# Time-warping distances with token tiles as the array's weights, and twenty identity matmuls as TensorE's first work

## The chip, the core and the metric

The kernel runs on one core of a Trainium2 chip. The core has TensorE (matmuls and transposes into PSUM), VectorE, ScalarE, GpSimd and SyncE, which only issues transfers, and they run beside each other and meet at semaphores. The metric is the device time of the whole program in microseconds; lower is better.

## The reference, cut to what matters

A block of two parts on tokens x (2 x 2048 x 512). The first aligns 154 context rows of each batch with the 2048 layer-normed tokens by dynamic time warping and adds every context row to the tokens that the path pairs it with. The second is a mixture of 8 linear experts with the top 2 of each token.

```python
D = sqrt(maximum(aa + bb - 2.0 * a @ b.T, 0.0))       # a: 154 context rows, b: 2048 normed tokens
R[i, j] = D[i, j] + min(R[i-1, j], R[i, j-1], R[i-1, j-1])
# backtrack R from its last corner; expanded[j] += a[i] for each cell (i, j) of the path
x = x + tanh(g_xattn) * expanded
w, sel = top_k(layernorm(x) @ gate_w.T, 2)
x = x + tanh(g_ffn) * sum over sel of softmax(w) * (layernorm(x) @ expert_w[sel].T)
```

## The kernel before

Tokens lie as 32 tiles of 128, in NG = 8 groups of GT = 4 tiles (512 tokens); the width of 512 is CH = 4 pieces of 128. The groups are worked in the order `ORDER`, from both ends of each sequence inwards, since the recurrence runs from both ends at once: the 154 context rows are two halves of H = 77, the second reversed. A **unit** of distances is one half of the context (h) of one batch (b) against one group of tokens (g); `UNITS` lists all NU = 16 in the order in which they are made.

**VectorE**, for each group: four statistics (`stats`, L715 and L719), a reciprocal (L725), four normalisations of a token tile into `stage` (`norm`, L731); after each second group the squared norms of the normed tokens in three bf16 pieces (`squared_norms`, L742 to L748). Then the values of the lanes (L757 to L779, with small borders), then the recurrence.

**TensorE** turns the context (L1415) and each group of `stage` (`transposes`, L1439: 16 fp32 transposes, one a weight load and a matmul against the identity). A unit (`products`, L1463) has the context as the weights, 80 or 104 columns of them, and 512 tokens as the moving side, summed over four pieces, two instructions a product. 104 columns are the second half of the context and, from column 96, eight rows of the centred gate, so that a unit with h = 1 gives the gate's logits too. Four small bf16 matmuls (L1473) add the squared token norms to each unit, after a turn of them (`bb_turn`, L1447). In the loop TensorE has transposes of group i, then unit i - 1; after the loop the other eight units follow on each other.

**ScalarE** copies the turned tokens to `big` (L1196), takes roots of the variances (`roots`, L1150), and for each unit does a relu with the context's squared norms as bias (`distances`, L1209) and a square root (L1215), for h = 1 a copy of the gate rows too (L1218). Between the last units it lays the codes of the traceback (`codes_laid`, L1250), then the table of tanh. **SyncE** loads the tokens, writes each unit's distances to memory (`distances_out`, L438) and reads them back skewed, in chunks of CS = 8 steps (`chunk`, L450, four transfers): chunk 0 asks for 4 units written, chunk 1 for 8, chunk 2 for 12, all later ones for 16. **GpSimd** sets constants, then waits until the groups are turned and splits the context into three bf16 pieces (L568 to L579, operations of 1 to 2 us), for the alignment at the end.

**The recurrence** has NS = 108 steps of five operations on VectorE (L793 to L806; L803 is the scan that reads the distances), beside which ScalarE and TensorE make the table of moves and turn the experts' weights (1 MB each, `stage` is their buffer). Behind it come the traceback (L818 to L883), the alignment, the gate and 78 tiles of experts (L1675, L1690), to the end.

## Time and profile before

| | |
|---|---|
| median of 3 runs | 637.68 us (637.3 to 638.35) |
| profiled execution | 639.95 us, span 638.2 us |
| busy PE / DVE / ACT / POOL | 490.0 / 298.9 / 250.3 / 237.6 us |
| chain that ended last, by engine | PE 60%, DVE 28%, DMA 4%, issue 3%, ACT 2% |

PE is TensorE's matmuls and PEld its weight loads, which overlap them; DVE is VectorE, ACT ScalarE, POOL GpSimd, SPq SyncE's queue. The page's chain follows the last instruction back to what released each step. L1690 (expert matmuls) is 40% of it, the products of the distances, L1463, 8%, the recurrence and the traceback most of VectorE's share. Busy shares are averages over stages that have different limits: the chain says which engine to read in which stage.

### The profile page before, as it was taken

What the parts mean: (1) busy time and instruction counts of PE and PEld (TensorE: products, weight loads), DVE (VectorE), ACT (ScalarE), POOL (GpSimd) and SP (SyncE); (2) the same over time, 40 slices, a digit from 0 to 9 for tenths busy, and PEclk for the clock granted to TensorE, in tenths of its full rate; (3) what the DMA queues carried; (4) which work ended last, traced back from release to release, by engine and by line L of the source; (5) the groups of instructions that cost most, each with busy time, mean ns of one, the idle gap of its engine ahead of it and who ended that gap; (6) DMA issues with size and microseconds to landing.
All of it is one profiled execution on the core that took longest, in us unless ns stands there. A gap on an engine that the chain in (4) does not pass through costs nothing.

```text
span 638.2 us, 7598 instructions
## 1 busy us (share of the span) xinstructions
PE 490.0 (77%) x1994; PEld 256.9 (40%) x2006; DVE 298.9 (47%) x1522; ACT 250.3 (39%) x460; POOL 237.6 (37%) x229
## 2 busy tenths in 40 slices
PE   3899997667700000474999899999999999999994
PEld 3554334445400000233545454444445444444441
DVE  7788974999998887799982400000000000000000
ACT  3665477464420000087578523222223332222221
POOL 4002903000000000012343356686677666766742
PEclk9899999896655555585999999999999999999998
DMA  9912524970007000375977966787787778777864
GB/s 297 372 33 69 163 59 125 261 187 20 2 0 263 1 1 5 133 275 173 311 217 185 356 129 109 136 164 137 134 159 138 137 135 158 122 137 136 153 101 61
DMA packets 56107, 91.76 MB, mean 144 GB/s; under 512 B 19263, under 2 KB 19263, under 8 KB 55907
## 3 DMA queue, kind: packets, MB, share of 16 engines
q0 software_dynamic: 18016, 43.00, 36.0%
q1 hardware_dynamic: 33056, 39.03, 18.9%
q10 hardware_dynamic: 4995, 9.25, 4.7%
q8 instruction: 18, 0.29, 0.2%
q14 instruction: 22, 0.18, 0.1%
HBM read 50.05 MB, written 41.21 MB: 143 GB/s over the span
## 4 chain that ended last, share of the span: by engine, by line
PE 60%; DVE 28%; DMA 4%; issue 3%; ACT 2%; SPq 1%; POOL 0%; ACTq 0%; POOLq 0%; DVEq 0%
PE psum L1690 40%; PE psum L1463 8%; DVE met L880 5%; PE psum L1675 5%; DVE waves L803 4%; DVE tokens L883 3%; DVE tokens L818 3%; PE psum L1439 2%; DVE tokens L946 2%; DVE shf L794 2%; PE psum L1617 2%; DVE tokens L806 1%; DMA am<-in_ctx_dram 1%; DMA tokens<-x_rows,gather_ids 1%; DVE tokens L797 1%
## 5 line engine op out<-in xcount | busy, mean ns | idle before, releaser
L1690 PE MATMUL psum<-big,tokens 128*128 x624 | 282.3, 596 | 0.2 <-ACT tokens L1371 0.2
L1690 PEld LDWEIGHTS psum<-big,tokens 128*128 128x128 f32 x624 | 113.1, 191 | 114.0 <-issue 114.0
L640 POOL DMA_INDIRECT tokens<-x_rows,gather_ids x78 | 77.8, 998 | 44.8 <-issue 23.0
L653 POOL DMA_INDIRECT out_dram<-work,add_ids x40 | 65.0, 1626 | 55.8 <-DMA out_dram<-work,add_ids 19.8
L653 POOL DMA_INDIRECT out_dram<-prow,add_ids x38 | 59.9, 1576 | 46.2 <-DMA out_dram<-work,add_ids 13.4
L1381 ACT ACTIVATE work<-psum,tile_shares 128x512 f32<-128x512 f32 x40 | 27.4, 686 | 101.2 <-PE psum L1690 95.2
L660 POOL DMA_DIRECT2D out_dram<-tokens x2 | 1.8, 910 | 168.7 <-DVE tokens L946 168.7
L1381 ACT ACTIVATE prow<-psum,tile_shares 128x512 f32<-128x512 f32 x38 | 26.0, 686 | 92.1 <-PE psum L1690 92.1
L1463 PE MATMUL psum<-big,aT 128*80 128x512 f32 (+1 forms) x128 | 60.3, 602 | 0.0
L1342 ACT ACTIVATE stage<-tokens,nm 128x512 f32<-128x512 f32 x32 | 21.6, 711 | 96.6 <-DVE tokens L946 96.6
L1585 PE MATMUL psum<-side,work 128*128 128x2 f32 x8 | 1.9, 356 | 70.6 <-DVE work L905 70.6
L1675 PEld LDWEIGHTS psum<-ident,tokens 128*128 128x128 f32 x312 | 38.6, 141 | 39.8 <-issue 35.9
L1371 ACT COPY tokens<-psum 128x512 f32<-128x512 f32 x78 | 45.1, 579 | 12.5 <-PE psum L1675 12.5
L1675 PE MATMUL psum<-ident,tokens 128*128 128x128 f32 x312 | 46.9, 273 | 2.0 <-DMA tokens<-x_rows,gather_ids 1.9
L803 DVE TENSOR_TENSOR_SCAN waves<-waves,shf,tokens 128x65 f32<-128x65 f32 x108 | 38.5, 357 | 12.7 <-DMA tokens<-dist_rows 12.7
L880 DVE SCALAR_TENSOR_TENSOR met<-tokens 128x70 bf16<-128x70 bf16 x108 | 31.5, 292 | 3.8
L1504 PE MATMUL psum<-ident,stage 128*128 128x128 f32 x128 | 20.0, 308 | 13.8 <-DMA stage<-in_L_ffn_expert_w_dram 11.0
L1585 PEld LDWEIGHTS psum<-side,work 128*128 128x128 f32 x8 | 1.8, 327 | 70.7 <-DVE work L905 70.7
L1617 PE MATMUL psum<-sm,prow 128*128 128x512 bf16 x90 | 28.5, 424 | 2.3 <-DVE tokens L946 1.6
L1463 PEld LDWEIGHTS psum<-big,aT 128*80 128x80 f32 (+1 forms) x128 | 18.7, 160 | 22.6 <-issue 21.2
L793 DVE TENSOR_TENSOR waves<-waves 128x64 f32<-128x64 f32 x108 | 27.2, 251 | 0.1
L946 DVE SCALAR_TENSOR_TENSOR tokens<-psum,tgates,tokens 128x512 f32<-128x512 f32 x32 | 22.3, 744 | 2.5 <-PE psum L1619 2.0
(322 smaller groups left out, 625.4 us busy)
## 6 DMA issues: line engine op xcount, KB each, us to landing
tokens<-in_x_dram SPq DMA_DIRECT2D x16, 1024.0 KB, 10.9
stage<-in_L_ffn_expert_w_dram ACTq DMA_DIRECT2D x8, 1024.0 KB, 7.4
x_rows<-stage SPq DMA_DIRECT2D x32, 256.0 KB, 2.6
out_dram<-tokens SPq DMA_DIRECT2D x6, 1024.0 KB, 7.9
tokens<-dist_rows SPq DMA_DIRECT2D x52, 64.0 KB, 3.1
dist_rows<-work SPq DMA_DIRECT2D x16, 160.0 KB, 2.0
out_dram<-tokens POOLq DMA_DIRECT2D x2, 1024.0 KB, 5.2
dist_rows<-prow SPq DMA_DIRECT2D x5, 256.0 KB, 11.1
```

The lines of the kernel that those rows point to most:

```text
L640: pool.indirect_dma_start(out=xin[:, n % UX, :], out_offset=None, in_=x2_d[b][:, :], in_offset=bass.IndirectOffsetOnAxis(ap=gids[:, b, j:j ...
L653: pool.indirect_dma_start(out=out_d.rearrange("b t c -> (b t) c"), in_=yout(n), in_offset=None, out_offset=bass.IndirectOffsetOnAxis(ap=ai ...
L793: v.tensor_tensor(mring[:, s % 3, 1:W1], up[:, 0:W], up[:, 1:W1], ALU.min).then_inc(s_min, 1)
L803: v.tensor_tensor_scan(own, mring[:, s % 3, :], dring[:, s // CS % DR, s % CS, :], shf[:, s % 2, 0:1], ALU.min, ALU.add).then_inc(s_row, 1)
L880: v.scalar_tensor_tensor(met[:, :], words[:, s + 1, :], words[:, s + 1, TW - 1:TW], itab[:, s, :], ALU.is_equal, ALU.mult, accum_out=words ...
L946: v.scalar_tensor_tensor(x[:, t, :], psum[:, bank(t), :], tgates[:, 0:1], x[:, t, :], ALU.mult, ALU.add).then_inc(s_x1, 1)
L1371: nc.scalar.copy(xinT[:, n % UX, :, :].rearrange("p c n -> p (c n)"), psum[:, n % UP, :]).then_inc(s_yc, 1)
L1381: nc.scalar.mul(yout(n), psum[:, UP + n % UP, :], scale[:, b, j:j + 1]).then_inc(s_ye, 1)
L1463: ins = nc.tensor.matmul(to[0:m, :], aT[:, b, c, h * H:h * H + m], xT[:, c, at:at + GW], start=(c == 0), stop=(c == CH - 1))
L1617: nc.tensor.matmul(psum[:, bank(t), :], pmain[:, b, cols], sm[:, b, j, 0:C], start=(j == 0), stop=False)
L1675: ins = nc.tensor.transpose(psum[:, n % UP, c * P:(c + 1) * P], xin[:, n % UX, c * P:(c + 1) * P], ident[:, :])
L1690: ins = nc.tensor.matmul(psum[:, UP + n % UP, :], xinT[:, n % UX, c, :], expT[:, bass.ds(own, 1), c, :].rearrange("p o d -> p (o d)"), sta ...
```

## The change

**Distances.** The raw token tiles are turned, not normed ones, and a group's products have 128 tokens as the weights and one row of 162 columns as the moving side: 154 context rows and 8 gate rows (`SG`). The context and the gate are centred instead (`ctx_centred`), so that the token means drop out. The products come out by token, so VectorE applies each token's scale and squared norm as it takes them out of PSUM (`squares_by_token`), and TensorE turns the 80 columns of each half back (`turned_back`) before ScalarE's relu and root. The normalisation into `stage`, the bf16 norm pieces and their matmuls, the gate-row copies on ScalarE and their turns on TensorE go. Both units of a group are made together, for all eight groups in `ORDER`.

**Order.** The main part of the context is loaded first, from SyncE. VectorE begins with the context, then the statistics of groups 0 and 1, the constants that it had set first (`borders`), and the statistics of group 2; the lane values stand between the fourth and fifth group. ScalarE has two units' work per group, two groups late; the codes are laid once between the last groups and three times behind them, and the loads of the first two experts are split. Chunk 0 asks for 8 units, all later chunks for 16. GpSimd splits the context as soon as its norms are there.

**First work.** The identity is made early, and TensorE begins with 20 fp32 matmuls of it by itself, 128 columns each, into PSUM bank 3, which transposes overwrite later.

```diff
@@ units of the distances, the width of a row of products @@
-    UNITS = [(b, g // 2, g) for g in (0, 3, 1, 2) for b in range(B)]
-    UNITS += [(b, h, g) for h, g in ((0, 2), (1, 1)) for b in range(B)]
-    UNITS += [(b, h, g) for h, g in ((0, 3), (1, 0)) for b in range(B)]
+    UNITS = [(i % B, h, ORDER[i] % GB) for i in range(NG) for h in range(2)]
...
-    GP = 96
-    HG = GP + E
+    SG = S + E
...
+        ctxc = stage[:, 0, :, :]
+        sq = stagef[:, GT * C:GT * C + 2 * GT * SG].rearrange("p (r k n) -> p r k n", r=2, k=GT)
...
+        AHEADS = 4
+        TR = (0, 1, 2, 3)
+        AT = (4, 5, 6, 7)
@@ SyncE @@
+            sp.dma_start(am[:, :, :], ctx_d[:, 0:SM, :].rearrange("b p c -> p b c")).then_inc(s_ctx, 16)
             for g in ORDER:
                 sp.dma_start(x[:, GT * g:GT * g + GT, :], x_v[g]).then_inc(s_x[g], 16)
-            sp.wait_ge(s_const, CONSTS)
+            sp.wait_ge(s_big, 1)
...
-                units = min(NU, 4 * (k + 1))
+                units = NU // 2 if k == 0 else NU
...
-            for u in range(7):
+            for u in range(NU // 2):
                 distances_out(u)
             sp.wait_ge(s_pad, 16 * (2 * B + 1))
-            sp.wait_ge(s_xn, GT * 7)
+            sp.wait_ge(s_tr, CH * (NG - 1))
+            sp.wait_ge(s_stat, GT * (NG - 1))
             chunk(0)
-            distances_out(7)
-            chunk(1)
-            for u in range(8, 12):
+            for u in range(NU // 2, NU):
                 distances_out(u)
-            chunk(2)
-            for u in range(12, NU):
-                distances_out(u)
-            for k in range(3, NC):
+            for k in range(1, NC):
                 chunk(k)
@@ GpSimd: the splitting of the context @@
-            pool.wait_ge(s_tr, CH * NG)
-            pool.wait_ge(s_xn, NT)
-            pool.wait_ge(s_ctx, 16)
-            pool.wait_ge(s_ctr, 48)
-            pool.wait_ge(s_ac, 2 * B)
-            pool.wait_ge(s_aT, 2 * B)
+            pool.wait_ge(s_cc, 2)
+            pool.wait_ge(s_aam, 1)
@@ VectorE @@
+            def ctx_centred(r):
+                a = am if r == 0 else ar[0:SR3, :, :]
...
+                for b in range(B):
+                    ins = v.bn_stats(cst[0:n, r, b, :], a[:, b, :])
+                link(ins)
+                for b in range(B):
+                    ins = v.bn_aggr(cmv[0:n, r, b, :], cst[0:n, r, b, :])
+                link(ins)
+                for b in range(B):
+                    ins = v.tensor_scalar(ctxc[0:n, 2 * r + b, :], a[:, b, :], cmv[0:n, r, b, 0:1], None, ALU.subtract)
+                ins.then_inc(s_cc, 1)
...
+                v.wait_ge(s_stat, GT * (i + 1))
+                link(v.tensor_scalar(bb[:, sl], mv[:, sl, 1], EPS, None, ALU.add))
+                link(v.reciprocal(bb[:, sl], bb[:, sl]))
+                link(v.tensor_scalar(bb[:, sl], bb[:, sl], -float(C) * EPS, float(C), ALU.mult, ALU.add))
...
+            def squares_by_token(i):
...
+                    if k % 2 == 0:
+                        v.wait_ge(s_d1, GT * i + k + 2)
+                    v.tensor_scalar(sq[:, i % 2, k, :], got, rstd[:, t:t + 1], bb[:, t:t + 1],
+                                    ALU.mult, ALU.add).then_inc(s_ev, 1)
+                    if k % 2:
+                        v.tensor_copy(xgs[:, t - 1:t + 1, :],
...
-                for k in range(GT):
-                    t = GT * g + k
-                    v.tensor_scalar(stage[:, i % 2, k, :], x[:, t, :], mv[:, t, 0:1], rstd[:, t:t + 1],
-                                    ALU.subtract, ALU.mult).then_inc(s_xn, 1)
...
-            for i in range(NG):
-                stats(i, range(GT))
-                norm(i)
-                if i % 2:
-                    squared_norms(i // 2)
+            link(v.memset(cmv[:, :, :, :], 0.0))
+            ctx_centred(0)
+            ctx_centred(1)
+            ctx_norms()
+            for i in range(2):
+                stats(i)
+            borders()
+            stats(2)
+            for i in range(AHEADS):
+                squares_by_token(i)
+                if i + 3 < NG:
+                    stats(i + 3)
...
+            for i in range(AHEADS, NG):
+                squares_by_token(i)
+                if i + 3 < NG:
+                    stats(i + 3)
@@ ScalarE @@
-                if h:
-                    at = (b * GB + g) * GW
-                    nc.scalar.copy(xg[:, at:at + GW], psum[GP:HG, 2 + u % 2, :]).then_inc(s_xgr, 1)
+            gate_centred()
             roots(0)
             for n in range(B):
                 context_turned(n)
-            for i in range(NG):
+            for c in range(CH):
+                copy(0, c)
+            for n in range(B, 2 * B):
+                context_turned(n)
+            roots(1)
+            for i in range(1, NG):
                 for c in range(CH):
                     copy(i, c)
...
+                if i >= 2:
+                    for h in range(2):
+                        distances(2 * (i - 2) + h)
+            act.dma_start(stage[:, 0, :, :], exp_v[0]).then_inc(s_w[0], 16)
...
-            for u in range(NG - 1, NU):
+            for u in range(NU - 4, NU):
                 distances(u)
-                if u >= NG + 1 and u < NG + 5:
-                    codes_laid(u - NG - 1)
+                if u == NU - 3:
+                    codes_laid(0)
+            act.dma_start(stage[:, 1, :, :], exp_v[1]).then_inc(s_w[1], 16)
+            for k in range(1, 4):
+                codes_laid(k)
@@ TensorE @@
-                pe.wait_ge(s_xn, GT * (i + 1))
+                pe.wait_ge(s_x[g], 16)
...
-                                                  stage[:, i % 2, k, c * P:(c + 1) * P], ident[:, :])
+                                                  x[:, GT * g + k, c * P:(c + 1) * P], ident[:, :])
...
+            def products(i):
+                b, at = ORDER[i] // GB, ORDER[i] * GW
+                pe.wait_ge(s_tra, CH * (i + 1))
+                for k in range(GT):
+                    if i and k % 2 == 0:
+                        pe.wait_ge(s_ev, GT * (i - 1) + k + 2)
+                        pe.wait_ge(s_xgs, 2 * (i - 1) + k // 2 + 1)
+                    to = psum[:, 4 + k // 2, k % 2 * SG:(k % 2 + 1) * SG]
+                    for c in range(CH):
+                        ins = nc.tensor.matmul(to, xT[:, c, at + k * P:at + (k + 1) * P], aT[:, b, c, :],
+                                               start=(c == 0), stop=(c == CH - 1))
+                    ins.then_inc(s_d1, 1)
+
+            def turned_back(i):
+                pe.wait_ge(s_ev, GT * (i + 1))
+                for h in range(2):
+                    if i:
+                        pe.wait_ge(s_dq, 2 * (i - 1) + h + 1)
+                    for k in range(GT):
+                        ins = nc.tensor.transpose(psum[0:HP, 6 + h, k * P:(k + 1) * P], sq[:, i % 2, k, h * H:h * H + HP],
+                                                  ident[:, :])
+                    ins.then_inc(s_d2, 1)
+
+            pe.wait_ge(s_ident, 1)
+            for _ in range(20):
+                nc.tensor.matmul(psum[:, 3, 0:P], ident[:, :], ident[:, :], start=True, stop=True)
...
+            transposes(1)
+            gate()
+            context_norms()
+            pe.wait_ge(s_gwc, B + 1)
+            pe.wait_ge(s_aab, 2)
+            for i in range(NG):
+                products(i)
+                if i:
+                    turned_back(i - 1)
+                if i + 2 < NG:
+                    transposes(i + 2)
+            turned_back(NG - 1)
```

The loop of TensorE, at a group in the middle of the distances. Before (`big` are the turned tokens, `prow` the norm pieces):

```order
L1439 MATMUL psum<-ident,stage 128x128 x16
L1463 MATMUL psum<-big,aT 104x512 x3
L1473 MATMUL psum<-prow 80x128 x4
L1463 MATMUL psum<-big,aT 104x512
L1439 MATMUL psum<-ident,stage 128x128 x16
L1463 MATMUL psum<-big,aT 80x512
```

After (here `stage` are the rows of distances by token, `tokens` the raw tokens):

```order
L1437 MATMUL psum<-aT,big 128x162 x16
L1447 MATMUL psum<-ident,stage 80x128 x8
L1424 MATMUL psum<-ident,tokens 128x128 x16
L1437 MATMUL psum<-aT,big 128x162 x16
L1447 MATMUL psum<-ident,stage 80x128 x8
```

One unit of four products stood behind each 16 transposes; now 16 short products and 8 transposes back stand there, for two units, and no units are left over for after the loop.

ScalarE at the end of the distances, relu and root by unit. Before:

```order
L1250 COPY tokens<-codes 128x28x66
L1209 ACTIVATE work<-psum,aam 80x512
L1215 ACTIVATE work<-work 80x512
L1209 ACTIVATE work<-psum,aab 80x512
L1215 ACTIVATE work<-work 80x512
L1218 COPY prow<-psum 8x512
L1209 ACTIVATE work<-psum,aab 80x512
L1215 ACTIVATE work<-work 80x512
L1218 COPY prow<-psum 8x512
L1298 ACT_TABLE_LOAD
```

After:

```order
L1228 DMA stage<-in_L_ffn_expert_w_dram 128x4x512
L1200 ACTIVATE work<-psum,ctx_norms 80x512
L1206 ACTIVATE work<-work 80x512
L1200 ACTIVATE work<-psum,aab 80x512
L1206 ACTIVATE work<-work 80x512
L1234 COPY tokens<-codes 128x27x66
L1200 ACTIVATE work<-psum,ctx_norms 80x512
L1206 ACTIVATE work<-work 80x512
L1200 ACTIVATE work<-psum,aab 80x512
L1206 ACTIVATE work<-work 80x512
L1242 DMA stage<-in_L_ffn_expert_w_dram 128x4x512
```

The four units of the last two groups now stand together behind TensorE's last products, with one laying of codes between them.

VectorE's first work. Before:

```order
L685 MEMSET eps 128x1
L686 MEMSET prow 32x2048
L688 MEMSET aT 128x8x27
L689 MEMSET lane_values 128x1
L691 MEMSET lane_values 31x1 x4
```

After:

```order
L701 BN_STATS ctx_stats<-am 128x6 x2
L704 BN_AGGR ctx_moments<-ctx_stats 128x2 x2
L707 TENSOR_SCALAR stage<-am,ctx_moments 128x512 x2
L701 BN_STATS ctx_stats<-ar 96x6 x2
L704 BN_AGGR ctx_moments<-ctx_stats 96x2 x2
L707 TENSOR_SCALAR stage<-ar,ctx_moments 96x512 x2
L712 TENSOR_TENSOR ctx_norms<-ctx_moments 128x4
L713 TENSOR_TENSOR ctx_norms<-ctx_norms,ctx_moments 128x4
L714 TENSOR_SCALAR ctx_norms<-ctx_norms 128x4
L721 BN_STATS st<-tokens 128x6 x4
```

The constants stood ahead of the first statistics of tokens; both parts of the context stand there now, and the constants follow two groups later.

## Rows read from the trace of the kernel before

**Rows 1.** Chain of waits, two units: start, us, what.

```profile
71.03 3.59 PE psum L1463 x8
74.97 3.59 PE psum L1463 x8
```

**Rows 2.** Chain of waits, the end of the distances (same columns).

```profile
97.86 0.43 PE psum L1463
...
99.70 0.69 ACT work L1209
...
101.07 1.96 DMA dist_rows<-work
```

**Rows 3.** VectorE in time: start, us, engine line op, out<-in, [idle before, releaser].

```profile
91.35 0.35 DVE L803 TENSOR_TENSOR_SCAN waves<-waves,shf,tokens 128x65 f32<-128x65 f32 x1 [3.34 <-DMA tokens<-dist_rows]
...
92.09 0.35 DVE L803 TENSOR_TENSOR_SCAN waves<-waves,shf,tokens 128x65 f32<-128x65 f32 x1
...
96.47 0.35 DVE L803 TENSOR_TENSOR_SCAN waves<-waves,shf,tokens 128x65 f32<-128x65 f32 x1
...
106.63 0.43 DVE L803 TENSOR_TENSOR_SCAN waves<-waves,shf,tokens 128x65 f32<-128x65 f32 x1 [9.34 <-DMA tokens<-dist_rows]
...
170.49 5.99 DVE L818 TENSOR_TENSOR_SCAN tokens<-tokens 128x2800 bf16<-128x2800 bf16 x1
```

**Rows 4.** TensorE's matmuls in time (as rows 3), transposes and the shortest fp32 product.

```profile
19.10 3.60 PE L1439 MATMUL psum<-ident,stage 128*128 128x128 f32 x16 [2.90 <-DVE stage L731]
...
39.33 1.97 PE L1439 MATMUL psum<-ident,stage 128*128 128x128 f32 x16
...
100.53 2.30 PE L1538 MATMUL psum<-aT,gwT 128*9 128x77 f32 x32 [0.22 <-ACT work L1209]
```

**Rows 5.** The weight loads of the same transposes, in time.

```profile
39.32 1.73 PEld L1439 LDWEIGHTS psum<-ident,stage 128*128 128x128 f32 x16 [0.99 <-DVE stage L731]
```

**Rows 6.** VectorE's groups by form, 0 to 100 us: xcount | busy us, mean ns.

```profile
L715 DVE BATCH_NORM_STATS2 st<-tokens 128x6 f32<-128x512 f32 x32 | 19.7, 679 | 1.0 <-DMA tokens<-in_x_dram 1.0
...
L731 DVE TENSOR_SCALAR stage<-tokens,mv,rstd 128x512 f32<-128x512 f32 x32 | 15.3, 543 | 0.3
...
L719 DVE BATCH_NORM_AGGREGATE mv<-st 128x2 f32<-128x6 f32 x32 | 3.0, 158 | 0.3
```

**Rows 7.** ScalarE's groups, same view.

```profile
L1196 ACT COPY big<-psum 128x512 f32<-128x512 f32 x32 | 16.7, 595 | 1.3 <-PE psum L1439 1.1
...
L1215 ACT ACTIVATE work<-work 80x512 f32<-80x512 f32 x15 | 9.5, 630 | 0.5
...
L1209 ACT ACTIVATE work<-psum,aab 80x512 f32<-80x512 f32 x8 | 5.5, 683 | 14.2 <-PE psum L1463 14.2
...
L1250 ACT COPY tokens<-codes 128x1782 bf16<-128x1782 bf16 x3 | 5.0, 1672 | 0.0
...
L1150 ACT ACTIVATE std<-mv,eps 128x4 f32<-128x4 f32 x8 | 2.4, 303 | 3.9 <-DVE mv L719 3.8
```

**Rows 8.** The start, in time: the first statistics, two context copies.

```profile
6.38 2.47 DVE L715 BATCH_NORM_STATS2 st<-tokens 128x6 f32<-128x512 f32 x4 [0.51 <-DMA tokens<-in_x_dram]
...
11.18 0.43 ACT L1159 ACTIVATE aT<-psum 128x308 f32<-128x308 f32 x1 [1.58 <-PE psum L1415]
...
12.36 0.34 ACT L1160 ACTIVATE aT<-psum 128x204 f32<-128x204 f32 x1
```

**Rows 9.** Chain of waits, the context's main part.

```profile
1.45 8.47 DMA am<-in_ctx_dram
```

**Rows 10.** TensorE by stretch: us, busy, granted clock, DMA share, GB/s.

```profile
19.10:22.20 3.10, 3.10 (x15) 0.50 1.05 387
```

**Rows 11.** GpSimd and VectorE side by side, in time.

```profile
60.17 1.04 POOL L568 CAST sm<-am 128x1024 bf16<-128x1024 f32 x1 [51.33 <-PE psum L1439]
60.24 0.98 DVE L764 TENSOR_TENSOR lane_values<-lane_values 128x1 f32<-128x1 f32 x1
...
62.40 2.13 POOL L577 TENSOR_TENSOR am<-am,sm 128x1024 f32<-128x1024 f32 x1
```

283 lines of the change are left out of this document (91 added, 192 removed).

## The prediction

> **What bounds the kernel now.** I read the chain of waits first, then the instructions of the engines at the places it names. From 10 to 101 us the chain lies on TensorE and just behind it: units of the distance product follow each other every 3.94 us, 3.59 us of it their own eight instructions [rows 1]. The last product ends just before 99.70, where the last relu on ScalarE begins; its square root, the write of the last distances and SyncE's reads follow [rows 2], and the step of the recurrence that needs them, step 24 of 108, begins its scan at 106.63 [rows 3]. So there are 7.0 us from the last product to that scan. VectorE had waited 3.34 us for the reads at step 16 and 9.34 us at step 24. From there the recurrence runs on VectorE to 170.49 [rows 3], and all behind it (traceback, alignment, experts) hangs on its end. What moves step 24 moves the end; behind it only small pieces that lie beside other work are edited.
>
> The kernel before has 24 steps done when the last distances arrive: its chunks of 8 steps ask for 4, 8, 12 and 16 units. The changed one has 8: chunk 0 asks for 8 units, every other for all 16. So the question is when step 8 starts after, plus 16 steps, against 106.63. Six steps from 92.09 to 96.47 are 0.73 us each [rows 3], so 16 are 11.7 us. **Break-even is step 8 at 94.9 us.**
>
> **TensorE's work.** A product instruction of 512 columns goes on for 0.43 us [rows 2], 0.84 ns a column, two instructions to a product. After, a group of 512 tokens is 16 products of 162 columns, 32 instructions, 0.136 us each if only the columns count. The nearest row of a short fp32 product, 77 columns, has 32 instructions in 2.30 us [rows 4], 0.072 each against 0.065 by columns: 7 ns more. I take 0.143 and 4.6 us a group; the lower bound is 0.136, 4.35 us. The weights are now 128 columns wide and new for every instruction. The transposes have the same 128x128 fp32 weights: 16 of them in 1.97 us [rows 4], their loads in 1.73 [rows 5], 0.108 a load, nearly all beneath the matmuls. So a load should not bind at 0.143. The bias matmuls (some 0.35 us of each 3.94, the difference in [rows 1]) and their turns go. Eight transposes back a group come at 0.12 each, 0.96 us. The transposes in remain, 1.93 us a group between their waits.
>
> One turn of the new loop is 4.6 + 0.96 + 1.93 = 7.5 us. In it VectorE has 2.47 us of statistics and 0.38 of aggregates [rows 6], three operations on four columns (0.6), a reciprocal, four evictions of 162 columns (by the 0.54 for 512 columns in [rows 6] 0.17 at least; I take 0.3, they read PSUM) and two small copies: 5.1 us. ScalarE has four copies (2.1), a root (0.3), two relus and two square roots with their gaps (2.7): 5.1 us [rows 7]. TensorE binds. With the lane values behind the fourth group (some 4.9 us if nothing blocks them) VectorE comes within 0.4 us of binding too; that is left in the range.
>
> **The start** decides how much of this is left. No product can begin before ScalarE has copied out the turned context and two groups of tokens, and ScalarE now has the root of group 0 ahead of all that. This waits for the statistics of group 0, which stand on VectorE behind both parts of the context. The main part, now first on SyncE, should land at about 5 us (1 MB of tokens, first before, had landed at 6.38 [rows 8]). The remaining 26 rows land between 5 and 12 us (before, the main part was under way for 8.47 us beside the tokens [rows 9]); I take 9. Centring them (two statistics, aggregates and subtractions) is 2.5 us, to 11.5; the norms 0.6, to 12.1; statistics of group 0 2.9, to 15.0; root, 15.3. Then ScalarE: four context copies 1.5 us [rows 8], four token copies 2.2, the rests of the context 0.5, a root 0.3, four token copies 2.1, gate and norms 0.7: **the first product begins at 22.7**. Of the clock: TensorE was granted 0.50, the 1.2 GHz level, from 19.10 to 22.20, after 2.90 us without work [rows 4, 10]. After, it idles from about 12.5 to 17, so I count part of the first group at 1.2 GHz, 1.5 us more, to 28.8; transposes of group 2, to 30.7. The products of group 1 also need group 0's first eviction. VectorE comes to it behind the statistics of group 1 (19.1), the constants that it set first before (4.5 us, 23.6) and the statistics of group 2 (27.1), if nothing blocks it.
>
> Something may. GpSimd's splitting of the context into bf16 pieces, from 60.17 on before, can now start at 12.1. In the trace a VectorE operation on 128x1 took 0.98 us and ended with the GpSimd copy beside it, and GpSimd's subtractions take 2.13 [rows 11]. Its whole splitting is 16 us. Two small operations of each group's statistics might wait like this, 0 to 5 us in all by 27 us. I put 1 us of it on the path: group 1's products begin at **31.7** (bounds 30.7 and 33.5).
>
> The Trainium skill, SBUF — State Buffer, section Who interferes with whom, says that a VectorE operation with two SBUF inputs, or one in a 2-port mode, is blocked for the whole of a GpSimd operation that holds the shared ports, and one with a single input outside those modes is not. [rows 11] agree on the first. By this rule token statistics and evictions from PSUM are never held, only small operations can be; the sum would be 1 us lower if none of those ran in a 2-port mode.
>
> The 20 matmuls of the identity (40 instructions) start at about 2.2 us and last 5 us at the high level of the clock, 9 at the low one, so until 11.3 at the latest. Nothing on the path asks TensorE for anything that can't be done by 15.3. They cost and gain nothing in this sum.
>
> **To the end.** Seven groups of products are 32.2 us, six lots of transposes back 5.8, five lots of transposes in 9.7: the last product ends at P = 31.7 + 47.7 = **79.4**. Behind it ScalarE is late, since it has nothing of the last two groups yet. From P + 0.55 it does relu, root, relu, root of group 6 (2.7), one laying of the codes (1.67), and the same 2.7 for group 7: P + 7.7 [rows 7]. Before, this tail was 1.4 us. The write takes 1.96 and the reads 3.6, as before [rows 2, 3]: step 8 at P + 13.3 = **92.7**. VectorE has steps 0 to 7 done by P + 8.2, hidden. Step 24 comes at 104.4 against 106.63, **2.2 us earlier**.
>
> Without a price, because hidden: on SyncE chunk 0 stands ahead of the writes of unit 8 on and asks for transposes of group 6, done by then. The gate-row copies on ScalarE, 32 small transposes on TensorE and one operation on VectorE go; all lay in the recurrence or beside the distances. Three layings of codes and the table of tanh move behind the distances, to P + 14.8 on ScalarE; the first move table can be asked for at P + 14, and VectorE needs it 24 steps later. The second expert's weights are loaded later, some 20 us before their turn.
>
> **Sum.** The profiled execution has a span of 638.2 us and took 639.95; the median of the runs is 637.68. The span becomes 638.2 - 2.2 = 636.0, the median 637.68 - 2.2 = **635.5**.
>
> **Rivals.**
> (a) *The weight loads don't hide under matmuls so short.* Then an instruction takes 0.108 + 0.136 = 0.244 us, a group 7.8, and eight groups 25 us more: 660 us. It decides from 0.153 us an instruction on (2.2 us over 224 instructions is 0.010 above 0.143). For it: no row of before has 128 new fp32 weight columns under an ordinary matmul of fewer than 512. Against it: 0.12 for transposes with the same loads [rows 4, 5]. Chance 6%. The Trainium skill, TensorE: Matmul & The Clock Gate, Part 3, says that a load overlaps a running matmul only where their row groups differ, which here they never do; it would give this rival. The transposes contradict it.
> (b) *The start eats the gain.* The 26 rows land at 12, or GpSimd holds VectorE for 5 us on the path, or both: group 1's products at 33.5 to 36.5. From 33.9 on it is slower than before, at 36.5 by 2.6 us: 637.3 to 640.3. Chance 23%.
> (c) *The start is quicker.* The 26 rows land early (1.5 us less), nothing blocks and the clock is up at once (1.5), a product instruction is 0.136 (1.5): 631 to 633. Chance 20%.
> (d) *The warm-up doesn't do what it is named for and the clock falls again in the loop*, for waits that I don't see: 10 us at 1.2 GHz cost 5 us, 640 to 643. The loop as worked out has no gap like the one before [rows 4, 10]. Chance 5%.
>
> **Numbers.** The forecast has 46% (its own range 633 to 637.3), the rivals the rest. What lies within 0.2% of before (1.3 us) a measurement of this kernel can't tell from no change. Faster by more: 0.62 (most of the forecast and all of c). Same: 0.16 (the forecast's end, half of b). Slower: 0.22 (a, d, half of b). The range of 631 to 641 holds the forecast, b, c and a part of d.
>
> **What would show it.** Product instructions at 0.143, a group in 4.6 us, loads beneath them; the first product at 22 to 23, the second group at 31 to 33; the last product near 79; ScalarE's last root 7.7 us later with a copy of codes between; the scan of step 8 at 92 to 93, after some 5 us idle on VectorE that a read of the distances ends; the recurrence's end at 168. I am wrong if TensorE waits inside the loop for evictions or relus, if the context lands late, or if what is behind the recurrence doesn't shift with it.

## The result: 4.95 us slower

| | before | after |
|---|---|---|
| median of 5 runs | 637.68 us (637.3 to 638.35) | 642.63 us (642.01 to 644.92) |
| profiled execution, span | 639.95, 638.2 | 642.63, 640.9 |
| last product ends | 99.7 | 80.7 |
| the scan that waited for the last distances | step 24 at 106.63 | step 8 at 97.95 |
| recurrence ends | 170.49 | 173.53 |

The ratio is 1.008, 95% interval 1.006 to 1.0101: slower by 0.8%, clear of noise, where 635.5 was forecast and 631 to 641 given as the range. The two profiled executions differ by 3.04 us at the end of the recurrence and by 2.7 in their spans; what lies behind the recurrence took 467.7 us before and 467.4 after. So the traces show 3 of the 4.95 us, and the chain up to step 8 is where to look. (The execution of before that was profiled took 2.3 us more than its median. Behind the recurrence, the eleven further executions profiled for this document took between 466.9 and 470.7 us, so a difference of 2 us there is within what single traces scatter by.)

The 3 us of the traces add up like this. TensorE's last product ends 19.0 us earlier. Of these, 11.7 us go to the 16 steps of the recurrence that had been done before the last distances came and now stand behind them. The stretch from the last product to the waiting scan has grown from 6.9 us (106.63 - 99.70) to 17.2 (97.95 - 80.72), another 10.3. That leaves 3.0 us lost. (Chunks that ask for fewer units, as before, were not tried.)

**TensorE** did more than was forecast. Instructions by form, 0 to 100 us, of after (count | busy us, mean ns | idle before, releaser), then one turn of its loop and the start of the next, in time (start, us, what):

```profile
L1437 PE MATMUL psum<-aT,big 128*128 128x162 f32 x256 | 39.7, 316 | 3.7 <-ACT gwT L1186 3.2 <-DVE x_gate L747 0.4
L1437 PEld LDWEIGHTS psum<-aT,big 128*128 128x128 f32 x256 | 38.3, 202 | 4.1 <-ACT gwT L1186 3.3 <-issue 0.4 <-ACT big L1191 0.4
```

```profile
42.23 4.58 PE L1437 MATMUL psum<-aT,big 128*128 128x162 f32 x32
46.65 1.03 PE L1447 MATMUL psum<-ident,stage 128*80 128x128 f32 x8
47.52 1.91 PE L1424 MATMUL psum<-ident,tokens 128*128 128x128 f32 x16
49.27 4.58 PE L1437 MATMUL psum<-aT,big 128*128 128x162 f32 x32
```

The loads lie wholly beside the matmuls: 32 instructions in 4.42 us from the first to the next group's work (46.65 - 42.23), 0.138 each, and a turn of 7.04 us instead of the 7.5 forecast. [rows 1] had 3.94 us a unit, 7.88 for two.

**The start** is late. The chain of waits of after (start, us, what), the long pieces of its first 36 us:

```profile
2.63 7.90 DMA ar<-in_ctx_dram
...
16.32 1.72 DVE bb L727
...
18.27 1.91 DVE bb L729
...
23.72 1.91 DVE bb L729
...
26.10 1.76 DVE prow L669
...
30.33 2.48 DVE st L721 x4
...
35.12 0.93 PE psum L1437 x5
```

GpSimd in time stands beside it, and VectorE's small operations, three beside GpSimd's work, one behind it:

```profile
15.87 2.13 POOL L557 TENSOR_TENSOR am<-am,sm 128x1024 f32<-128x1024 f32 x1
18.08 2.06 POOL L559 TENSOR_TENSOR ar<-ar,srs 96x1024 f32<-96x1024 f32 x1
```

```profile
16.32 1.71 DVE L727 TENSOR_SCALAR bb<-mv 128x4 f32<-128x4 f32 x1
...
18.27 1.89 DVE L729 TENSOR_SCALAR bb<-bb 128x4 f32<-128x4 f32 x1
...
23.12 0.35 DVE L727 TENSOR_SCALAR bb<-mv 128x4 f32<-128x4 f32 x1
...
33.67 0.17 DVE L729 TENSOR_SCALAR bb<-bb 128x4 f32<-128x4 f32 x1
```

The operation at 16.32 ends at 18.03, just as GpSimd's subtraction ends (18.00); the one at 18.27 ends at 20.16, as the next one does (20.14). The same holds for the two of group 1, which end at 23.47 and 25.62 where operations of GpSimd end at 23.45 and 25.59. Four operations that take 0.17 us alone took 5.85 us together; the reciprocal between each two (0.18 us) did not grow. Behind them the constants (from 26.10) and the statistics of group 2 (from 30.33) also stood ahead of the first eviction, which the products of group 1 need. ScalarE and TensorE follow (in time):

```profile
16.32 0.30 ACT L1157 ACTIVATE std<-mv,eps 128x4 f32<-128x4 f32 x1 [7.83 <-DVE mv L724]
...
23.12 0.30 ACT L1157 ACTIVATE std<-mv,eps 128x4 f32<-128x4 f32 x1 [3.17 <-DVE mv L724]
```

```profile
2.47 7.17 PE L1453 MATMUL psum<-ident 128*128 128x128 f32 x40 [2.47 <-POOL ident L498]
9.47 1.04 PE L1398 MATMUL psum<-ident,stage 128*128 128x128 f32 x8
10.35 1.91 PE L1424 MATMUL psum<-ident,tokens 128*128 128x128 f32 x16
...
18.32 3.37 PE L1424 MATMUL psum<-ident,tokens 128*128 128x128 f32 x16 [4.57 <-ACT big L1191]
...
25.74 7.47 PE L1437 MATMUL psum<-aT,big 128*128 128x162 f32 x32 [3.25 <-ACT gwT L1186]
```

The turned context and group 0 stood ready in PSUM at 12.3, and ScalarE's queue held them behind the root of group 0 until 16.3, then group 1's copies behind its root until 23.1. TensorE idled 4.57 and 3.25 us; its first product group took 7.47 us, mostly at the 1.2 GHz level (the granted clock of 25.70 to 33.10 was 0.61). Group 1's transposes ended at 34.96, and its products waited 0.16 us more for VectorE: the two paths came out almost equal.

**The end of the distances.** The chain of after again, from the last product:

```profile
80.72 0.45 PE psum L1447 x4
...
88.15 0.64 ACT work L1206
88.81 5.58 DMA dist_rows<-work
...
95.81 2.12 DMA tokens<-dist_rows
```

The last write took 5.58 us; the last one of before took 1.96 [rows 2]. ScalarE in time shows what was issued 0.65 us ahead of it, and the same request stood at 60.14 before, in the middle of the distances (the second fence is of before):

```profile
88.16 0.38 ACTq L1242 DMA_DIRECT2D stage<-in_L_ffn_expert_w_dram  x1
```

```profile
60.14 1.01 ACTq L1233 DMA_DIRECT2D stage<-in_L_ffn_expert_w_dram  x2
```

VectorE then has, against 106.63 and 170.49 in [rows 3]:

```profile
97.95 0.35 DVE L815 TENSOR_TENSOR_SCAN waves<-waves,shf,tokens 128x65 f32<-128x65 f32 x1 [9.58 <-DMA tokens<-dist_rows]
...
173.53 5.99 DVE L830 TENSOR_TENSOR_SCAN tokens<-tokens 128x2800 bf16<-128x2800 bf16 x1
```

Step 8 at 97.95 plus 16 steps of 0.73 is 109.65, 3.02 later than 106.63, and the recurrence ends 3.04 later: the break-even rule (step 8 at 94.9) held within 0.02 us.

### The profile page after: what moved, and what is told of

It is laid out like the page before. It is cut to its first block, busy times and chain, and to the rows that moved or that the text cites. A ratio compares the mean times of both kernels' runs of the same rounds, so it can differ in the third digit from the quotient of the medians.

```text
span 640.9 us, 7873 instructions
## 1 busy us (share of the span) xinstructions
PE 475.6 (74%) x2126; PEld 283.1 (44%) x2138; DVE 294.9 (46%) x1544; ACT 241.7 (38%) x443; POOL 235.9 (37%) x227
## 4 chain that ended last, share of the span: by engine, by line
PE 54%; DVE 33%; DMA 5%; issue 4%; ACT 2%; POOL 0%; SPq 0%; ACTq 0%; POOLq 0%; DVEq 0%
PE psum L1653 39%; DVE met L892 5%; PE psum L1638 5%; DVE waves L815 4%; PE psum L1437 4%; DVE tokens L895 3%; DVE tokens L830 3%; DVE shf L806 2%; DVE tokens L818 2%; DVE tokens L809 2%; PE psum L1580 2%; DVE st L721 2%; DMA ar<-in_ctx_dram 1%; DVE waves L805 1%; DVE tokens L954 1%
## 5 line engine op out<-in xcount | busy, mean ns | idle before, releaser
L622 POOL DMA_INDIRECT tokens<-x_rows,gather_ids x78 | 79.5, 1019 | 46.3 <-issue 22.5
L635 POOL DMA_INDIRECT out_dram<-work,add_ids x40 | 63.2, 1579 | 54.8 <-DMA out_dram<-work,add_ids 20.1
L1437 PE MATMUL psum<-aT,big 128*128 128x162 f32 x256 | 39.7, 316 | 3.7 <-ACT gwT L1186 3.2
L1437 PEld LDWEIGHTS psum<-aT,big 128*128 128x128 f32 x256 | 38.3, 202 | 4.1 <-ACT gwT L1186 3.3
L1491 PE MATMUL psum<-columns,eye 128*128 128x512 bf16 (+1 forms) x14 | 6.6, 470 | 26.9 <-DVE tokens L818 26.7
L805 DVE TENSOR_TENSOR waves<-waves 128x64 f32<-128x64 f32 x108 | 24.4, 226 | 0.1
```

What stands on the lines that cost most here:

```text
L622: pool.indirect_dma_start(out=xin[:, n % UX, :], out_offset=None, in_=x2_d[b][:, :], in_offset=bass.IndirectOffsetOnAxis(ap=gids[:, b, j:j ...
L635: pool.indirect_dma_start(out=out_d.rearrange("b t c -> (b t) c"), in_=yout(n), in_offset=None, out_offset=bass.IndirectOffsetOnAxis(ap=ai ...
L805: v.tensor_tensor(mring[:, s % 3, 1:W1], up[:, 0:W], up[:, 1:W1], ALU.min).then_inc(s_min, 1)
L1437: ins = nc.tensor.matmul(to, xT[:, c, at + k * P:at + (k + 1) * P], aT[:, b, c, :], start=(c == 0), stop=(c == CH - 1))
```

## The experiments

All times are ratios to the kernel before on the same chip; its medians on the three chips used were 638.9 to 639.3. The changed kernel itself was measured at 1.008. The half width of their intervals is 0.0015 to 0.0027, 1.0 to 1.7 us, so the traces carry the finer steps.

**The second expert's weights, moved (a_e1_late).**

```diff
-            act.dma_start(stage[:, 1, :, :], exp_v[1]).then_inc(s_w[1], 16)
             for k in range(1, 4):
                 codes_laid(k)
+            act.dma_start(stage[:, 1, :, :], exp_v[1]).then_inc(s_w[1], 16)
```

> The changed kernel, with one line moved: ScalarE asks for the second expert's weights (1 MB) behind the last three layings of the codes instead of ahead of them. Theory 1 (the last write of distances took 5.58 us instead of 1.96 because that transfer was put into the queues 0.65 us ahead of it): the last write takes 2.0 us again, the scan of step 8 begins near 94.3 instead of 97.95, and the time falls by 3.6 us, to about 639.0. Theory 2 (the write is slow because it comes last from a ScalarE that lays codes, or for another reason that has nothing to do with the weights): the write stays near 5.6 us and the time at 642.6. Theory 3 (the transfer only collides with something later, the reads of the next chunks): the write is short, step 8 at 94.3, but VectorE waits for a chunk of distances further on, and less than 2 us of the 3.6 is left.

1.0077 [1.0051, 1.0104], and the last write took 5.37 us. By its number theory 2, but ScalarE in time shows that the edit did not do what it says:

```profile
88.37 0.38 ACTq L1244 DMA_DIRECT2D stage<-in_L_ffn_expert_w_dram  x1
88.89 4.87 ACT L1234 COPY tokens<-codes 128x1782 bf16<-128x1782 bf16 x3
```

The request, behind three copies in the program, was issued 0.5 us before the first of them began. It waited for nothing of them, so this run doesn't tell the theories apart.

**The same with a wait (a2_e1_gated).**

```diff
             for k in range(1, 4):
                 codes_laid(k)
+            act.wait_ge(s_code, 4)
+            act.dma_start(stage[:, 1, :, :], exp_v[1]).then_inc(s_w[1], 16)
```

> The changed kernel, with the request for the second expert's weights (1 MB) behind the last three layings of the codes and a wait for their ends ahead of it. (Moved without that wait it was issued at 88.37 us, ahead of the layings all the same, and the last write took 5.37 us.) Theory 1 (the last write of distances takes 5.58 us because that transfer is put into the queues 0.65 us ahead of it): the last write takes 2.0 to 2.2 us, the scan of step 8 begins near 94.5 instead of 97.95, the recurrence ends 3.4 us sooner, and the time falls by 3.4 us, from 1.0075 of the kernel before to 1.002. Theory 2 (the write is slow for a reason of its own): it stays above 5 us, and the time at 1.0075 of before. Theory 3 (the collision only moves to the reads of the next chunks): step 8 comes at 94.5, a later chunk late, and less than 2 us remain.

1.0014 [0.9997, 1.0032], that is 4 us less than 1.0077 and no longer distinguishable from the kernel before. The chain and ScalarE in time:

```profile
90.00 1.96 DMA dist_rows<-work
...
95.35 6.48 DMA tokens<-dist_rows
```

```profile
94.78 0.41 ACTq L1245 DMA_DIRECT2D stage<-in_L_ffn_expert_w_dram  x1
```

The write is back at 1.96 us. This execution had a start that was 0.92 later (group 1's products at 36.04) and yet step 8 at 95.49 and the end of the recurrence at 171.42, 2.1 us sooner; with an equal start that is 3.0. The transfer now meets the read of the next chunk, which took 6.48 us, and VectorE waited 0.44 us for it at 101.85. (The kernel before has such a meeting too: a read of 6.24 us at 106.41, behind a request for 1 MB at 106.35.) Theory 1, with a little of theory 3.

**GpSimd's splitting held back (c_split_late).**

```diff
             pool.wait_ge(s_cc, 2)
             pool.wait_ge(s_aam, 1)
+            pool.wait_ge(s_tr, CH * NG)
+            pool.wait_ge(s_stat, NT)
```

> The changed kernel, with GpSimd's splitting of the context held back until all transposes in and all token statistics are done, as before the change. Theory 1 (GpSimd's copies and subtractions hold back VectorE's small operations on four columns, 5.1 us of them in the start, and 3.4 of that stand ahead of the root of group 1 and so ahead of the first product): those operations take 0.17 us each, the first product begins at 22.3 instead of 25.74, group 1's at 31.7 instead of 35.12, the last product ends at 77.3 instead of 80.72, and the time falls by 3.4 us, to 639.2, if the splitting does no harm where it lies then. Theory 2 (the small operations are slow for another reason, their place behind the aggregates): they stay at 1.7 to 1.9 us and nothing moves. Theory 3 (the clock, at 1.2 GHz for the first group, sets group 1's start anyway): the first product comes 3.4 us sooner, the second group less than 1.5 us sooner.

1.0017 [0.9996, 1.0037], no different from before; the recurrence ended at 170.88, 2.65 sooner, though the rest of the context landed 0.4 later. VectorE and TensorE in time:

```profile
17.13 0.17 DVE L731 TENSOR_SCALAR bb<-bb 128x4 f32<-128x4 f32 x1
```

```profile
23.88 6.76 PE L1439 MATMUL psum<-aT,big 128*128 128x162 f32 x32 [0.29 <-issue]
...
32.23 4.58 PE L1439 MATMUL psum<-aT,big 128*128 128x162 f32 x32
```

Theory 1: the four small operations take 0.17 us each, group 1's products come at 32.23 instead of 35.12. The splitting, from 68.27 now, blocks VectorE there instead; a step's first operation at 80.31, 0.22 us elsewhere, took 2.13. It was hidden, since steps 0 to 7 wait for nothing else and step 8 still idled 5.05 us.

**The warm-up taken away (b_no_warm), and put alone into the kernel before (h_before_warm).** The second also sets the identity right behind its memset, as the change does.

```diff
-            for _ in range(20):
-                nc.tensor.matmul(psum[:, 3, 0:P], ident[:, :], ident[:, :], start=True, stop=True)
```

> The changed kernel without the 20 matmuls of the identity. Theory 1 (they bring nothing, since TensorE then waits from 13.8 to 18.3 us and the first group of products runs at 1.2 GHz all the same): the first eight context transposes and the 16 of group 0 take about twice as long, 2.1 and 3.5 us, but end before 15 us, well ahead of ScalarE's first copy at 16.5; the first product stays at 25.7 and the time within 0.5 us of 642.6. Theory 2 (they keep a later clock up): the first group's products, 7.47 us now, become longer, up to 8.9 us, and the time rises by up to 1.4 us. Theory 3 (without them the clock is no worse and ScalarE or the queues gain): the time falls by over 1 us.

> The kernel before, with the 20 matmuls of the identity alone as TensorE's first work (the identity is set right behind its memset, as in the changed kernel; the bank is the one that the second context transposes overwrite). Theory 1 (the warm-up is worth nothing here either: TensorE waits for VectorE again before its first long run of transposes): the transposes of group 1 at 19.1 us stay at 3.6 us, the step 24 scan stays at 106.6, the time within 0.7 us of 637.7. Theory 2 (in the kernel before the clock comes up for the context and group 0, which lay at 1.2 GHz from 10.1 to 15.5 us): up to 1.5 us less on the way to the first product, 636.2. Theory 3 (early consts are later by the identity's 0.2 us and TensorE's 7 us of work collide with its first real work at 10 us): up to 0.5 us slower.

1.0073 [1.0049, 1.0098] without it, against 1.008 with it; 1.0003 [0.9986, 1.0019] for the kernel before with it. TensorE in time, without the warm-up in the changed kernel:

```profile
7.77 1.94 PE L1398 MATMUL psum<-ident,stage 128*128 128x128 f32 x8 [7.77 <-DVE stage L707]
9.51 3.47 PE L1424 MATMUL psum<-ident,tokens 128*128 128x128 f32 x16
...
26.06 6.32 PE L1437 MATMUL psum<-aT,big 128*128 128x162 f32 x32 [2.72 <-ACT gwT L1186]
```

and with it in the kernel before:

```profile
10.03 1.07 PE L1421 MATMUL psum<-ident,am 128*128 128x128 f32 x8 [1.49 <-DMA am<-in_ctx_dram]
...
18.98 3.59 PE L1445 MATMUL psum<-ident,stage 128*128 128x128 f32 x16 [2.90 <-DVE stage L733]
```

Theory 1 twice, by the times. The warm-up halves what follows at once (the context's transposes take 1.04 or 1.07 us instead of 1.94) and nothing later; without it these can start 1.7 us earlier, at 7.77, so that group 0 stands in PSUM at 13.0 instead of 12.3, and ScalarE comes at 16 either way. (Without it step 8 of this execution came at 98.81, 0.86 later; 0.3 of that was there at group 1's products. The two medians differ by less than their intervals.)

**The lane values later (l_lanes_later).**

```diff
-        AHEADS = 4
+        AHEADS = 6
```

> The changed kernel, with VectorE's lane values (some 20 small operations, 4.3 us) behind the sixth group's evictions instead of the fourth's, where no token statistics stand beside them. Theory 1 (they are what TensorE waits for ahead of the fifth group's products, which begin at 63.74 where the loop's turn of 7.0 us puts them at 62.1): that group's products begin at 62.1, the last product ends at 79.1 instead of 80.7, the time falls by 1.6 us. Theory 2 (the wait is of another kind and goes to the sixth or seventh group): the last product ends at 80.7 again, the time stays.

1.0075 [1.0061, 1.009]. The products of group 4 began at 63.27, 7.03 behind group 3's, where the changed kernel has 7.44 between the two, so the wait was there, but it was 0.4 us and not 1.6: I had counted the turns along the chain of waits, which has no piece for the products of group 3 (56.30). The gain was gone again by step 8 (97.93), with a wait of ScalarE for a write and 5.71 us of the last write. Theory 2 by its result, theory 1 by its place.

**The start alone in another order (s_start_order).**

```diff
@@ ScalarE @@
             gate_centred()
-            roots(0)
             for n in range(B):
                 context_turned(n)
...
             for n in range(B, 2 * B):
                 context_turned(n)
-            roots(1)
+            roots(0)
...
                     context_norms_turned()
+                    roots(1)
@@ VectorE: the three operations on bb (L727 to L729) go from stats(i) to the start of squares_by_token(i) @@
             for i in range(2):
                 stats(i)
-            borders()
             stats(2)
             for i in range(AHEADS):
                 squares_by_token(i)
+                if i == 1:
+                    borders()
```

> The changed kernel with its start alone put in another order (the roots of groups 0 and 1 behind the copies on ScalarE, the weights from the variances just ahead of each group's evictions, the constants behind group 1's evictions); codes, expert weights and lane values stay as the change has them. If the late root of group 0 and the small operations are what the start costs: first product near 19.3 instead of 25.7, group 1's at 25.5 to 26.8 instead of 35.1, the last product near 73 instead of 80.7, the last write again above 5 us, step 8 near 90.3, and the time 7.7 us lower than the changed kernel's (0.996 of before). Rival: the tail behind the last product grows as the writes of distances now fall together with other traffic, and less than 5 us of it remains.

0.9962 [0.9947, 0.9977]: 7 us less than the 1.0073 to 1.008 of the changed kernel and the three runs that left its time as it was, and the recurrence ended at 166.59, 6.9 sooner. First product and group 1's, then the last write:

```profile
18.98 6.32 PE L1438 MATMUL psum<-aT,big 128*128 128x162 f32 x32 [2.49 <-ACT gwT L1187]
...
26.88 4.58 PE L1438 MATMUL psum<-aT,big 128*128 128x162 f32 x32
```

```profile
81.78 5.59 DMA dist_rows<-work
```

As expected; step 8 at 90.91. This edit alone makes the change a gain of 0.4%. It moves three things at once (the roots, the small operations, the constants), and no run shows what each of them gives.

**Everything (f_all), and the first expert's weights late too (f2_all_e0).** The start as above; `AHEADS = 6`; the second expert's weights with their wait; and

```diff
             for u in range(NU - 4, NU):
                 distances(u)
-                if u == NU - 3:
-                    codes_laid(0)
+            codes_laid(0)
             for k in range(1, 4):
                 codes_laid(k)
             act.wait_ge(s_code, 4)
+            act.dma_start(stage[:, 0, :, :], exp_v[0]).then_inc(s_w[0], 16)    # f2_all_e0 only, moved from its place ahead of unit 12
             act.dma_start(stage[:, 1, :, :], exp_v[1]).then_inc(s_w[1], 16)
```

> The changed kernel with everything that the traces point to. ScalarE takes the root of group 0 behind the context copies and group 0's copies, and that of group 1 behind the gate and norm copies; VectorE computes the weights from the variances just ahead of each group's evictions, sets the constants behind group 1's evictions and the lane values behind group 5's; all four layings of the codes stand behind the last distances, and the second expert's weights are asked for when they are done. If the start, the lane values, the codes and the write cost what the traces say: first product near 20 us instead of 25.7, group 1's near 28 instead of 35.1, last product at 72 instead of 80.7, last write begins at 78.5 instead of 88.8 and takes 2.0, step 8 at 84.1 instead of 97.95, the recurrence ends 13.8 us sooner, and the time is 629, 0.984 of the kernel before. Rival: VectorE, with the small operations blocked by GpSimd until 30 us and the constants behind group 1, becomes late for the groups 1 to 3 and gives back 3 to 5 us (632 to 634); or steps 0 to 7 are not done when the reads land, from step 8 at 82 on.

> The kernel just described, with the first expert's weights too asked for only behind the codes. Theory 1 (a square root of ScalarE waits some 1.0 to 1.6 us for an earlier write of distances that goes on beside this transfer): those waits go, step 8 comes 1 to 2 us sooner than in the kernel just described (82 to 83), the time is 1 to 2 us lower (627.5). Theory 2 (the write of 2 us itself, not the transfer, makes the root wait, since there are two buffers): no change. Theory 3 (the first expert's turn now starves, and with it ScalarE's move tables): VectorE waits in the recurrence, up to 4 us slower.

0.9872 [0.9855, 0.9888] and 0.9862 [0.9839, 0.9884]. In the first, the last write began at 79.80 and took 1.97 us, step 8 came at 85.33 and the recurrence ended at 160.96. An earlier write met the first expert's transfer, and a root of ScalarE waited for it (chain of f_all, then ScalarE in time):

```profile
70.47 5.83 DMA dist_rows<-work
```

```profile
76.38 0.63 ACT L1207 ACTIVATE work<-work 80x512 f32<-80x512 f32 x1 [1.31 <-DMA dist_rows<-work]
```

With that transfer late too, step 8 was at 84.11, 1.2 us sooner, though group 1's products had begun 1.2 us later (26.77 against 25.55). TensorE then waited 9.6 us in all for experts' weights, 3.6 at most, where in f_all it waited for none; but VectorE, which carries the path there, waited for nothing behind step 8, and the recurrence took 75.63 us from step 8 in both. In the times the two can't be told apart. Both fell short of what was expected (f_all 630.77 us against 629; the other 630.43 against 627.5, step 8 at 84.11 against 82 to 83). VectorE was late for group 3 in both (products at 41.6), as the rival had it.

**The constants in three parts (f4_borders), and without the warm-up (f5_no_warm).**

```diff
-                if i == 1:
-                    borders()
+                if 1 <= i <= 3:
+                    borders(i)      # 1: the pad rows, 2: edge and rings, 3: the other lane constants
```

> The kernel with everything (second expert's and first expert's weights late), with VectorE's constants in three parts behind the evictions of groups 1, 2 and 3. In it the products of group 3 began at 41.6 where the loop's turn of 7.03 us puts them at 40.9 (in the run with the quicker start, at 39.6). Theory 1 (the constants in one piece make VectorE late there): group 3's products come at 39.6 to 40.9, step 8 and the time come 0.6 to 2.0 us sooner, 628.5 to 630. Theory 2 (VectorE has too little left in each turn, and only the place of the wait moves): no change.

> The same kernel as the one just described, without the 20 matmuls of the identity. Theory 1 (now that ScalarE takes the copies first, the start hangs on TensorE's transposes, and the clock counts): the transposes of group 1 take 3.6 us instead of 1.97, the first product comes 0.8 us later and its group takes 6.3 us instead of 4.65, group 1's products come up to 2 us later, and the time rises by 1 to 2 us. Theory 2 (they are hidden, as in the changed kernel): within 0.5 us of it.

0.9836 [0.9817, 0.9855] and 0.9839 [0.9821, 0.9857], in intervals that overlap with that of f2_all_e0: medians of 627.79 and 628.18 us where before had 639.01. The first beats both kernels of this document, by 1.6% the one before. Its chain, then VectorE in time:

```profile
77.92 1.97 DMA dist_rows<-work
```

```profile
83.50 0.35 DVE L820 TENSOR_TENSOR_SCAN waves<-waves,shf,tokens 128x65 f32<-128x65 f32 x1 [3.76 <-DMA tokens<-dist_rows]
...
159.09 5.99 DVE L835 TENSOR_TENSOR_SCAN tokens<-tokens 128x2800 bf16<-128x2800 bf16 x1
```

Group 3's products begin at 41.12 after 27.04, 34.08: turns of 7.04 with no wait, theory 1; step 8 comes 0.6 us sooner than in f2_all_e0 (83.50 against 84.11), the least that was expected. Without the warm-up the start was not slower but quicker (group 1's products at 24.84 against 27.04). TensorE in time, without it:

```profile
9.50 3.62 PE L1429 MATMUL psum<-ident,tokens 128*128 128x128 f32 x16
...
13.91 1.97 PE L1429 MATMUL psum<-ident,tokens 128*128 128x128 f32 x16
18.61 4.65 PE L1442 MATMUL psum<-aT,big 128*128 128x162 f32 x32 [1.93 <-ACT gwT L1191]
```

Work that the kernel needs anyway brought the clock up by 13.91; theory 1 has fallen and the warm-up is worth nothing here either; the medians are the same within their intervals. (The profiled execution of this kernel was its slowest, 631.42 us: a root of ScalarE waited 6.85 us for the first write of distances, which went on beside the pad rows, and TensorE waited 1.80 for ScalarE. With the warm-up the same root waited 3.89 us and TensorE nothing.)

## Why the prediction was wrong, step by step

Forecast and trace for step 8: 92.7 and 97.95, 5.25 us apart. By the sum's own terms: start +3.4, loop -2.1, ScalarE's tail +0.4, the last write +3.6, the reads 0.

- **The last write, 1.96 forecast, 5.58 measured: the term that failed most.** The step reads "The write takes 1.96 and the reads 3.6, as before", and in the next paragraph "The second expert's weights are loaded later, some 20 us before their turn" stands among what has no price because it is hidden. I asked who waits for the moved transfer, and not what it runs beside. Taking that transfer away from it (a2_e1_gated) gave 3 us in the trace and 4 in the time.
- **The start, 31.7 forecast with bounds of 30.7 and 33.5, 35.12 measured.** Rival (b) with its "GpSimd holds VectorE for 5 us" was what happened, at a price of 5.2 us in four operations. I had the mechanism and the row, [rows 11], and took 1 us of it. No row stood behind taking so little: the two operations of each group stand behind the statistics while GpSimd works without a break from 13.64 to 29.9, so each will meet a copy or a subtraction. The run with the splitting held back gave 2.9 us at group 1's products. The constants and the statistics of group 2 behind them, which the sum had ended at 27.1, ended at 33.8. The rest is smaller: the 26 rows of context landed at 10.5 (9 taken), and the first group ran at the low clock nearly throughout, 7.47 us, where 6.1 was taken, after 4.57 and 3.25 us without work. (ScalarE's pieces in the sum add up to a first product at 22.6, not 22.7; nothing hangs on it.)
- **That ScalarE's order mattered** stood in the forecast ("ScalarE now has the root of group 0 ahead of all that"), as a part of the start's sum; that it is a choice and no need is what I did not see. With the roots behind the copies, and the small operations and constants out of the way, the time fell by 7 us, where the recurrence ended only 2.65 us sooner with the small operations alone unblocked.
- **The loop was right and better:** 0.138 us an instruction where 0.143 was taken, turns of 7.04 where 7.5 was. Some 0.18 us of a turn lie in the products, the rest in the transposes, which I had added by the spans of their rows, and these overlap their neighbours. Rival (a) is refuted: loads of 128 fresh columns hid under matmuls of 0.138 us. So is the rule of the Trainium skill (TensorE: Matmul & The Clock Gate, Part 3) that was cited for it, that a load overlaps a running matmul only where their row groups differ. The trace disagrees with it in 256 instructions. (The same part also lets a load run ahead that goes to a background weight buffer. That would fit; no run here shows where a load went.)
- **The other cited rule,** of the Trainium skill, SBUF — State Buffer, section Who interferes with whom, agrees: statistics (0.68 us before [rows 6] and after) and evictions from PSUM (0.80 us for two, in f_all beside GpSimd's work too) never grew, the operations with a scalar on four columns out of SBUF did, and the reciprocals did not. What I did not take from it is that "small" says nothing of the price: each is held for the rest of GpSimd's operation, up to 2 us.
- **The lane values**, left in the range, cost TensorE 0.4 us. **The tail** of ScalarE was 7.7 forecast, 8.1 measured. In it a root waited 0.99 us for a write of 5.51 us, issued at 78.51, 0.65 us behind the request for the first expert's weights: the same collision, once more and cheaper.
- **The warm-up at nothing** was right: with and without it in three kernels, each pair within its intervals.
- **What followed the recurrence** shifted with it, as forecast. Where the other 1.9 us of the medians comes from stays open: before, on other chips, the same program took 639 and kernels with the changed kernel's path 643.4 to 643.9, so the difference is 4.1 to 4.8 there, while their recurrences ended 3.0 to 4.0 later. It may be only that stretches of 467 to 471 us behind it scatter.

The sign was thus decided by two numbers: I took the write at its shortest, without asking for an upper bound, and the blocked operations near the lower end of their range. With the write at 1.96 and all else as measured, step 8 would stand at 94.3, below the break-even of 94.9. With the blocked operations at 0.17 us instead, by c_split_late, at 95.25: either one alone brings the change back to no difference (1.0014 and 1.0017). Both together, 3.6 and 2.7 us off 97.95, would put step 8 at 91.6 if they add up, 3.3 us below break-even and near the 92.7 of the forecast (whose loop was 2.1 us too slow); that was not run by itself.

## What to carry to other kernels

When an edit moves a large transfer, ask what else is being transferred at its new place, not only when its data is needed: 1 MB issued 0.65 us ahead of the last write of a chain made that write 3.6 us longer. When GpSimd work on wide operands is released earlier, count each small SBUF operation of VectorE of the kinds that grew here (a tensor with a scalar, two tensors) at the rest of the GpSimd operation beside it, and put those operations where nobody waits for them. On an in-order engine, put what waits for the slow producer (here roots behind statistics) behind what is ready. With that and the small operations and constants moved, the change that was 0.8% slower became 0.4% faster; with the transfers, the codes and the lane values moved as well, 1.6%.

## What the runs showed of the hardware

- A transfer's request on ScalarE's queue doesn't wait for the copies ahead of it in the program: it was issued at 88.37, the copies began at 88.89 and took 4.87 us. Only a wait for their semaphore held it back (94.78).
- The last write of distances took 1.96 or 1.97 us where no transfer of 1 MB stood beside it (before, a2_e1_gated, f_all and the three after it) and 5.37 to 5.71 us where one had been asked for 0.65 us ahead of it (the changed kernel and five runs). A write met by the first expert's transfer took 5.83 us in f_all and 6.09 in b_no_warm; a read of distances 2.1 us alone and 6.24 or 6.48 beside such a transfer.
- The granted clock of the first product group differed between executions of kernels with the same start. After 2.48 to 2.50 us without work it was at the 2.4 GHz level throughout in one (f_all, 4.65 us the group) and part of the time at 1.2 GHz in three (6.20 to 6.32 us); after 1.93 us it stayed high, after 3.25 us the group took 7.47. The time without work just ahead is not all of it: in c_split_late the group began 0.29 us behind other work and took 6.76 us. That work began with 16 transposes at the low level (3.64 us, against 1.91 at the high one), after 4.56 us without any. The windows of two of these, f_all at the full clock and f4_borders (start:end us, length, TensorE, loads, VectorE, ScalarE, GpSimd busy, clock, DMA share, GB/s):

```profile
19.00:25.00 6.00, 5.68 (x43) 5.71 (x44) 5.79 (x21) 1.37 (x8) 5.73 (x5) 1.00 1.05 386
```

```profile
19.00:25.40 6.40, 6.26 (x33) 6.29 (x34) 5.63 (x19) 0.63 (x4) 6.13 (x5) 0.73 1.05 388
```
